# Sorting tokens to experts: integer compares, shifted prefix sums, one product on ScalarE, two peels issued later

## The reference

```python
xn = layernorm(x)                                   # 8 x 512 x 128
# attention: 8 heads of 16; differential: out1 - lam * out2, layernorm, times 0.2, Wo
s = attention(xn, Wq, bq, Wk, bk, Wv, bv, Wo, bo, lambdas, ln_w, ln_b)
# experts: the group h of a token comes from its first two numbers
h = mod((xn[:, 0] + xn[:, 1]).astype(int32), 8)     # cast cuts off towards zero
sel = [h, mod(h + 1, 8)]                            # two of eight experts, half weight each
f = mean over e in sel of (relu(xn @ W1[e] + b1[e]) @ W2[e] + b2[e])
out = x + s * silu(f)
```

## Time and profile before

| | us |
|---|---|
| median of 3 runs | 412.05 (411.11 to 412.3) |
| the profiled execution, its own time | 411.52 |
| its span, first to last instruction | 409.6 |
| PE busy in the span | 381.5 (93%) |
| DVE busy | 291.8 (71%) |
| ACT busy | 267.5 (65%) |
| POOL busy | 189.3 (46%) |
| mean granted TensorE clock | 0.991 of full |

### The profile page before, as it was taken

How to read it: one execution, slowest core, us unless ns; L and a number is a source line. 1 busy time by engine, 2 the same in 40 slices (tenths; PEclk the granted TensorE clock), 3 DMA queues, 4 the chain that set the end, 5 groups by cost and what they waited for, 6 DMA issues and landing times.

```text
span 409.6 us, 8427 instructions
## 1 busy us (share of the span) xinstructions
PE 381.5 (93%) x2576; PEld 248.3 (61%) x2576; DVE 291.8 (71%) x758; ACT 267.5 (65%) x667; POOL 189.3 (46%) x262
## 2 busy tenths in 40 slices
PE   4996989999999999999999999999999999999993
PEld 2353876565775667766665668765676667764321
DVE  7787996656686757766676767866686767866884
ACT  3581756666765776576666767676766668675783
POOL 7944203454456543565355532663573444541200
PEclk9996999999999999999999999999999999999999
DMA  7975953263216451265105640346136141216740
GB/s 263 343 230 112 242 196 91 80 206 105 79 37 191 111 195 21 79 190 168 46 27 170 189 140 18 136 121 197 48 127 216 22 169 47 81 26 213 230 159 26
DMA packets 36945, 54.75 MB, mean 134 GB/s; under 512 B 6724, under 2 KB 25141, under 8 KB 36903
## 3 DMA queue, kind: packets, MB, share of 16 engines
q1 hardware_dynamic: 31456, 46.94, 34.6%
q0 software_dynamic: 3296, 6.76, 7.8%
q10 hardware_dynamic: 2151, 0.53, 0.6%
HBM read 15.59 MB, written 6.75 MB: 55 GB/s over the span
## 4 chain that ended last, share of the span: by engine, by line
PE 74%; DVE 7%; DMA 5%; ACT 4%; SPq 4%; issue 4%; POOL 1%; ACTq 0%; DVEq 0%; POOLq 0%
PE ring L1393 14%; PE pv_bank L1327 13%; PE ring L1414 12%; PE score L1289 12%; PE exp L1314 10%; PE ring L1251 3%; DVE neg_max L1049 3%; DMA xs<-xn_rows,inverse 3%; SPq L532 2%; PE ring L1335 2%; PE ring L1255 1%; PE ring L1353 1%; PE ring L1276 1%; PE ring L1375 1%; PE score L1264 1%
## 5 line engine op out<-in xcount | busy, mean ns | idle before, releaser
L1049 DVE TENSOR_REDUCE neg_max<-score 128x1 f32<-128x512 f32 x256 | 169.0, 683 | 72.3 <-PE score L1289 66.7
L1289 PE MATMUL score<-ks,qs 96*128 96x512 bf16 x256 | 98.3, 386 | 6.3 <-DVE neg_max L1049 6.0
L787 ACT ACTIVATE probs<-exp 128x512 f32<-128x512 f32 x124 | 72.5, 605 | 36.3 <-PE exp L1314 32.3
L787 ACT ACTIVATE xin<-exp 128x512 f32<-128x512 f32 x120 | 69.7, 604 | 38.5 <-PE exp L1314 38.1
L1314 PE MATMUL exp<-qs,ks 99*128 99x512 bf16 x244 | 91.7, 380 | 0.1
L825 ACT ACTIVATE hT<-ring,pair 128x128 f32<-128x128 f32 x256 | 73.4, 377 | 13.0 <-PE ring L1393 11.9
L1414 PEld LDWEIGHTS ring<-w_sb,hT 128*128 128x128 f32 x568 | 73.5, 191 | 10.4 <-issue 3.5
L1414 PE MATMUL ring<-w_sb,hT 128*128 (+1 forms) x568 | 75.4, 275 | 0.9 <-ACT hT L825 0.9
L1393 PEld LDWEIGHTS ring<-xsT,pair 128*128 128x128 f32 x512 | 66.3, 191 | 14.6 <-issue 8.1
L1393 PE MATMUL ring<-xsT,pair 128*128 128x128 f32 x512 | 68.2, 276 | 1.7 <-issue 1.2
L684 POOL TENSOR_SCALAR tanh<-tanh 128x128 f32<-128x128 f32 x32 | 17.2, 536 | 95.5 <-ACT tanh L845 95.2
(11 more groups left out here) (198 smaller groups left out, 417.4 us busy)
## 6 DMA issues: line engine op xcount, KB each, us to landing
pair<-table SPq DMA_DIRECT2D x32, 580.0 KB
qs<-parts SPq DMA_DIRECT2D x42, 128.0 KB
ks<-parts SPq DMA_DIRECT2D x42, 128.0 KB
xin<-_attn_hidden_states_dram SPq DMA_DIRECT2D x8, 256.0 KB, 4.4
table<-in_L_ffn_W_dram SPq DMA_DIRECT2D x2, 1024.0 KB, 9.2
w_sb<-in_L_ffn_W_dram SPq DMA_DIRECT2D x8, 256.0 KB, 10.4
xn_rows<-xn SPq DMA_DIRECT2D x8, 256.0 KB, 3.0
table<-_attn_hidden_states_dram SPq DMA_DIRECT2D x8, 256.0 KB, 5.4
```

What stands on the lines that cost most here:

```text
L787: a.activation(prob(n), exp_banks[n][:, :], ACT.Exp, scale=SCALE).then_inc(exp_done, 1)
L1049: v.tensor_reduce(neg_max[:, b % 2, col:col + 1], score_bank[n % 2][:, :], AX.X, ALU.max, negate=True).then_inc(max_taken, 1)
L1289: t.matmul(score_bank[n % 2][:, :], qs[0:MAX_ROW, b % STK, hh, c * P:(c + 1) * P], ks[0:MAX_ROW, b % STK, hh, :], start=True, stop=True).t ...
```

## The change

In the list of steps: `peel 1 0 2` goes behind `score 4`, `peel 1 1 2` behind `score 5`; before, both stood ahead of `invert`. `tokens` goes ahead of `bias_copy` and has a part on ACT now. `extras` and `groups 2` go ahead of one score each on DVE. The extra tiles' `turn_tile` (f = 1 and 3 to 6) goes ahead of one or two steps on PE and ACT. `tanh` of the tiles f = 11, 12, 17, 18, 24, 25, 31, 32, 37 and 38 goes behind one `exp` on ACT, that of f = 21 behind `turn_z`. The moves of `split_max` and `load_y_init` pass no step of their own engines, so no engine's program changes by them.

In the grouping: the mean's part is subtracted from the pair's sum before the reciprocal deviation is there, so that one product is left behind it; the casts back to f32 are gone, and comparisons read the integers; `onehot` and `seen` lie one word further to the front, so that the scan reads one place off and gives the sum without the token's own one; `token[1]` is written by ACT. In the layer norm of batches 4 to 7, POOL subtracts the mean and multiplies, so `shift` isn't formed for them.

```diff
-PEEL_AT = (((-55.5, -55.3), (-55.4, -55.25)), ((-45.5, -45.3), (-45.4, -45.2)))
+PEEL_AT = (((-55.5, -55.3), (-55.4, -55.25)), ((-45.5, 4.5), (-45.4, 5.1)))
-TOKENS_AT = -45
+TOKENS_AT = -45.46
-EXTRAS_AT = 5.2
-GROUPS_AT = (9.05, 10.72, 13.05, 14.05)
+EXTRAS_AT = 4.7
+GROUPS_AT = (9.05, 10.72, 12.55, 14.05)
-TX, DX = 2.4, 3.2
+TX, DX = 3, 3.2
-INIT_AHEAD = 1.5
+INIT_AHEAD = 1.67
-SPLIT_MAX, TURN_MAX = 16.8, 18.9
+SPLIT_MAX, TURN_MAX = 16.5, 18.9
-TANH, GATE = 0.7, 1.84
+TANH, GATE = 1, 1.84
...
-        onehot = work[:, 512:768].rearrange("p (e t) -> p e t", e=EXP)
-        seen = work[:, 768:1024].rearrange("p (e t) -> p e t", e=EXP)
+        onehot = work[:, 511:767].rearrange("p (e t) -> p e t", e=EXP)
+        seen = work[:, 767:1023].rearrange("p (e t) -> p e t", e=EXP)
...
-                    if end < B:
+                    if first not in POOL_NORM:
...
-                    pool.wait_ge(shift_ready, 1 + [b >= end for _, end in LN_GROUPS].index(False))
+                    pool.wait_ge(rstd_ready, 1 + [b >= end for _, end in LN_GROUPS].index(False))
                     for t in range(C * b, C * b + C):
-                        last = g.tensor_scalar(xn[:, t, :], xin[:, t, :], rstd[:, t:t + 1], shift[:, t:t + 1],
-                                               ALU.mult, ALU.add)
+                        last = g.tensor_scalar(xn[:, t, :], xin[:, t, :], mv[:, t, 0:1], rstd[:, t:t + 1],
+                                               ALU.subtract, ALU.mult)
...
+                elif kind == "tokens":
+                    act.wait_ge(in_tile_ready, 1)
+                    a.activation(token[:, 1, :, :, :], in_tile, ACT.Copy, scale=row_of[:, 0:1]).then_inc(token_ready, 1)
...
                 dve.wait_ge(pair_summed, 1)
+                dve.wait_ge(rstd_ready, len(LN_GROUPS))
                 link(v.tensor_tensor(v01[:, :], v01[:, :], rstd[:, :], ALU.mult))
-                dve.wait_ge(shift_ready, len(LN_GROUPS))
-                link(v.scalar_tensor_tensor(v01[:, :], shift[:, :], 2.0, v01[:, :], ALU.mult, ALU.add))
...
-                link(v.tensor_copy(n_abs[:, :], whole_i))
-                link(v.tensor_tensor(over, n_abs[:, :], v_abs[:, :], ALU.is_gt))
-                link(v.tensor_tensor(n_abs[:, :], n_abs[:, :], over, ALU.subtract))
-                link(v.scalar_tensor_tensor(h[:, :], sign[:, :], -1.0, n_abs[:, :], ALU.add, ALU.mult))
-                link(v.tensor_copy(whole_i, h[:, :]))
-                link(v.tensor_scalar(whole_i, whole_i, EXP - 1, None, ALU.bitwise_and))
-                link(v.tensor_copy(h[:, :], whole_i))
+                link(v.tensor_tensor(over, whole_i, v_abs[:, :], ALU.is_gt))
+                link(v.tensor_tensor(n_abs[:, :], whole_i, over, ALU.subtract))
+                link(v.scalar_tensor_tensor(h_i[:, :], sign[:, :], -1.0, n_abs[:, :], ALU.add, ALU.mult))
+                link(v.tensor_scalar(h_i[:, :], h_i[:, :], EXP - 1, None, ALU.bitwise_and))
...
-                flat = work[:, 768:1024]
-                link(v.tensor_tensor_scan(flat, work[:, 512:768], zeros,
-                                          0.0, ALU.add, ALU.add))
-                v.tensor_tensor(seen[:, :, :], seen[:, :, :], onehot[:, :, :], ALU.subtract).then_inc(seen_ready, 1)
+                v.tensor_tensor_scan(work[:, 768:1024], work[:, 511:767], zeros,
+                                     0.0, ALU.add, ALU.add).then_inc(seen_ready, 1)
...
-                v.tensor_tensor(token[:, 0, :, :, :], in_tile, by_pair(ordinal[:, :], FT), ALU.mult)
-                v.tensor_scalar(token[:, 1, :, :, :], in_tile, row_of[:, 0:1], None, ALU.mult).then_inc(token_ready, 1)
+                dve.wait_ge(in_tile_ready, 1)
+                v.tensor_tensor(token[:, 0, :, :, :], in_tile, by_pair(ordinal[:, :], FT), ALU.mult).then_inc(token_ready, 1)
...
-                    v.tensor_tensor(v01[:, :], xin[:, :, 0], xin[:, :, 1], ALU.add).then_inc(pair_summed, 1)
-                    dve.wait_ge(rstd_ready, g + 1)
+                    link(v.tensor_tensor(v01[:, :], xin[:, :, 0], xin[:, :, 1], ALU.add))
                     dve.wait_ge(stats_ready, end)
-                    v.scalar_tensor_tensor(shift[:, tok], mv[:, tok, 0], -1.0, rstd[:, tok],
-                                           ALU.mult, ALU.mult).then_inc(shift_ready, 1)
+                    v.scalar_tensor_tensor(v01[:, :], mv[:, :, 0], -2.0, v01[:, :],
+                                           ALU.mult, ALU.add).then_inc(pair_summed, 1)
...
-                    pe.wait_ge(token_ready, 1)
+                    pe.wait_ge(token_ready, 2)
```

More of the change, by code:

```diff
@@ L306, in gated_attention_moe @@
         sign = sb("sign", [P, NT])
-        h = sb("h", [P, NT])
+        h_i = sb("h_i", [P, NT], I32)
         count = sb("count", [P, EXP])
@@ L429, in gated_attention_moe @@
         token_ready = sem("token_ready")
+        in_tile_ready = sem("in_tile_ready")
         slots_split = sem("slots_split")
@@ L860, in _ @@
             v.memset(zeros, 0.0)
+            v.memset(work[:, 767:768], 0.0)
             link(v.memset(va[:, :, :, :, HD:VW], 0.0))
@@ L896, in count_groups @@
                 v.tensor_scalar(sign[:, :], v01[:, :], 0.0, 2.0, ALU.is_ge, ALU.mult)
-                link(v.tensor_copy(n_abs[:, :], whole_i))
-                link(v.tensor_tensor(over, n_abs[:, :], v_abs[:, :], ALU.is_gt))
-                link(v.tensor_tensor(n_abs[:, :], n_abs[:, :], over, ALU.subtract))
-                link(v.scalar_tensor_tensor(h[:, :], sign[:, :], -1.0, n_abs[:, :], ALU.add, ALU.mult))
-                link(v.tensor_copy(whole_i, h[:, :]))
-                link(v.tensor_scalar(whole_i, whole_i, EXP - 1, None, ALU.bitwise_and))
-                link(v.tensor_copy(h[:, :], whole_i))
-                link(v.tensor_tensor(onehot[:, :, :], h[:, :].unsqueeze(1).to_broadcast([P, EXP, NT]),
+                link(v.tensor_tensor(over, whole_i, v_abs[:, :], ALU.is_gt))
+                link(v.tensor_tensor(n_abs[:, :], whole_i, over, ALU.subtract))
+                link(v.scalar_tensor_tensor(h_i[:, :], sign[:, :], -1.0, n_abs[:, :], ALU.add, ALU.mult))
+                link(v.tensor_scalar(h_i[:, :], h_i[:, :], EXP - 1, None, ALU.bitwise_and))
+                link(v.tensor_tensor(onehot[:, :, :], h_i[:, :].unsqueeze(1).to_broadcast([P, EXP, NT]),
                                      iota[:, 0:EXP].unsqueeze(2).to_broadcast([P, EXP, NT]), ALU.is_equal))
                 v.tensor_reduce(count[:, :], onehot[:, :, :], AX.X, ALU.add).then_inc(count_ready, 1)
-                flat = work[:, 768:1024]
-                link(v.tensor_tensor_scan(flat, work[:, 512:768], zeros,
-                                          0.0, ALU.add, ALU.add))
-                v.tensor_tensor(seen[:, :, :], seen[:, :, :], onehot[:, :, :], ALU.subtract).then_inc(seen_ready, 1)
+                v.tensor_tensor_scan(work[:, 768:1024], work[:, 511:767], zeros,
+                                     0.0, ALU.add, ALU.add).then_inc(seen_ready, 1)
             def make_slots(fill, shared):
@@ L945, in find_tokens @@
                 dve.wait_ge(slots_split, 1)
-                link(v.tensor_tensor(in_tile, by_pair(slot_tile[:, 0:NT], FT), over_pairs(columns[:, :, :], NT // 2), ALU.is_equal))
-                v.tensor_tensor(token[:, 0, :, :, :], in_tile, by_pair(ordinal[:, :], FT), ALU.mult)
-                v.tensor_scalar(token[:, 1, :, :, :], in_tile, row_of[:, 0:1], None, ALU.mult).then_inc(token_ready, 1)
+                v.tensor_tensor(in_tile, by_pair(slot_tile[:, 0:NT], FT), over_pairs(columns[:, :, :], NT // 2),
+                                ALU.is_equal).then_inc(in_tile_ready, 1)
+                dve.wait_ge(in_tile_ready, 1)
+                v.tensor_tensor(token[:, 0, :, :, :], in_tile, by_pair(ordinal[:, :], FT), ALU.mult).then_inc(token_ready, 1)
             def find_rows(q):
@@ L1014, in _ @@
                         continue
-                    tok = slice(C * first, C * end)
-                    v.tensor_tensor(v01[:, :], xin[:, :, 0], xin[:, :, 1], ALU.add).then_inc(pair_summed, 1)
-                    dve.wait_ge(rstd_ready, g + 1)
+                    link(v.tensor_tensor(v01[:, :], xin[:, :, 0], xin[:, :, 1], ALU.add))
                     dve.wait_ge(stats_ready, end)
-                    v.scalar_tensor_tensor(shift[:, tok], mv[:, tok, 0], -1.0, rstd[:, tok],
-                                           ALU.mult, ALU.mult).then_inc(shift_ready, 1)
+                    v.scalar_tensor_tensor(v01[:, :], mv[:, :, 0], -2.0, v01[:, :],
+                                           ALU.mult, ALU.add).then_inc(pair_summed, 1)
                 elif kind == "transpose_x" and s[1] not in PEELED:
```

## The result

The changed kernel takes 417.38 us (median, 416.79 to 417.61), the kernel before on the same chip 411.58. The ratio is 1.0146, 95% interval 1.0108 to 1.0184: slower by 5.8 us. The prediction had said 411.5 and a range to 413.6. The profiled execution of the changed kernel took 417.56, its span is 415.8.

A forecast was written before the change was run, and what follows sets the result against it. TensorE held 74% of the chain, but what counted was the time before about 70 us, with DVE rigid from 40 to 62. Terms -1.1 + 0.6 = -0.5 gave 411.0, as median 411.5; range 410.0 to 413.6.

The forecast's parts named there:

- The POOL part: POOL's layer norm of batches 4 and 5: two products fewer, gain at most 0.05 us.
- Removed on DVE, worth nothing: DVE's grouping ahead of make_slots: small instructions go, counts ready about 1 us earlier, but PE's count matmul sets it; gain 0.
- its cover: PE's peels of batch 0, said to hide the DVE and POOL savings; without them worth 1.5 us.
- The product on ScalarE: token[1]'s product moved from DVE to ACT at 26.72: takes 1.3 us there, ends DVE's at_row pieces 0.45 us earlier.
- the 1.04: Product on ACT and two peels moved behind the inversion: first gather starts and lands 1.04 us earlier, bounds 0.5 to 1.2.
- Rival (c): ACT's transfers start only after the late peel 1 1 1 copy and end at 37.4: 412.2 us, chance 0.12.
- The row-based forecast: ACT's fifteen transfers taken to start when they did before, from 29.33 to 36.92, with the peels' copies behind them.
- The clock: PE from 34 to 38 us: the moved first peel keeps full clock, so hidden 0 ends 1.2 us earlier.
- rival (b): PE's clock falls before turn_tile 0, second peel at half speed on the path, hidden 0 1.6 us later: 414.2, chance 0.16.
- The tanh moves: ACT's tanh in eleven tiles: gain 0, at best 0.5; tile 12's delays tile 14's gather, costing 0 to 0.85, taken 0.6.
- The sum without the form: Forecast total: -1.1 + 0.6 = -0.5 us against the profiled 411.52, so 411.0; as median 411.5.
- the first term: -1.1 us: hidden 0 ends earlier, taken between 1.2 at full clock and 0.9 if ACT's transfers delay the peel's copy.

The follow-up runs named there:

- the old form: Changed kernel with POOL's normalise of batches 4 to 7 put back to product and addition, shift formed again: 408.82 us against 409.97 of before, ratio 0.9974.
- the mended one: Changed kernel with minus_mean formed on POOL and added where the mean was subtracted: 410.86 us against 411.46 of before, ratio 0.9997.
- the second run with the old form: Changed kernel with POOL's product and addition back, run once more on another chip in more rounds: 408.95 us, ratio 0.9985.

## Why the prediction was wrong

**The step that failed is this:** "The POOL part is alike: two products fewer ... Gain at most 0.05." I costed the two small products that go and not the sixteen large instructions whose form changes. The trace of before has no subtraction of this shape on POOL, so the form was an operation that had to be bounded from both sides. I took it as the same operation, and the row of those sixteen instructions wasn't even among my rows. With double their 8.2 us POOL would have ended at 33, and by the earlier trace rows the stores about 3 us after that. That rival, some 5 us slower, could have been worked out from the trace, and it had no chance in the text. Measured, the form took 14.9 us in place of 8.2, the stores came last at the gather where the prediction had put the inversion, and the time grew by 5.8 us.

**Removed on DVE, worth nothing:** right for the execution it was read from, too general as a rule. With the steps gone, DVE waited for PE's counts ahead of `make_slots` for 0.3 to 1.3 us in five profiles (0.87 in the changed kernel) and not at all in three. With them in, PE waited for DVE by 0.4 and 0.6 us in two. PE's matmul of the counts stood anywhere from 20.05 to 22.10. The prediction itself said that both ends had met by chance; its cover was as uncertain. What the steps are worth in the median isn't shown.

**The product on ScalarE:** right in size. It started at 26.84 and took 1.33 us, against 1.3. It was in nobody's way, but only because the peels had moved. Its share of the gather is 0.47, from one execution of each; the 1.04 that I gave the edit together with the peels came out as 0.96 with the old form (31.45 to 30.49), 0.25 of it from PE being that much earlier at the counts.

**Rival (c), ACT's transfers behind the late copy:** wrong. ACT's queue in the changed kernel:

```profile
26.84 1.33 ACT L754 ACTIVATE probs<-hT,row_of 128x1248 bf16<-128x1248 bf16 x1
26.86 0.35 ACTq L719 DMA_DIRECT2D lams<-in_L_attn_lambda_q_dram  x1
```

The first of the transfers starts 0.02 us after the product, though five instructions of ACT's stand between them in its program and run only from 28.06 on. The row-based forecast had them at 29.3 or later. By the Trainium skill, "Advanced Engine Details and Errata" (Engine Queue Depths), ScalarE's queue holds 8 instructions, so its sequencer can hand over the product and the copies and go on; the trace agrees. The other half of that step held: a copy behind the transfers does wait for them. ACT in the run with the old form alone:

```profile
31.56 2.45 ACTq L732 DMA_DIRECT2D ks<-ones_bf  x3
34.06 0.69 ACT L778 ACTIVATE probs<-ring,qk_bias 128x512 bf16<-128x512 f32 x1 [4.57 <-PE ring L1260]
```

The profile names PE, but PE's matmul was over at 33.71 and the last transfer at 34.01. It cost nothing, as the first tile came only at 34.92. The transfers are thirteen, not the fifteen of the prediction.

**The clock:** the forecast of full clock from 34 to 38 held with the old form in some traces and not in others. Of the eight profiles with the old form or the mended one and the peels moved, three had 1.00 from 24 to 44 all the way (the first with the old form alone, and those with the product or the grouping back). In the others it fell for some microseconds between 28 and 38. In the second run with the old form the price was about 0.6 us and not 1.6, as the clock had mostly come back before the second peel (0.93 in the window from 36 to 38). In the changed kernel the gather was so late that the fall came behind it too, and there the second peel did run at half clock on the path, by the mechanism of rival (b).

**The tanh moves:** the gather of tile 14 was issued later as foreseen (129.09; by the 4.94 us of the shift it would have been 128.2), but it landed earlier too, and PE was 0.53 us less behind at that tile, not 0.6 more. So the lower bound, 0, was the right end for this term of the sum; that other traffic sets the landing is not shown. Over the whole stretch from tile 8 to the last, the shift against the profile of before grew by 1.2 us in the changed kernel. In the others it goes with the chip and not with the steps. On the two chips where the kernel before took 410.0 and 409.8 us, in all seven profiles it went down by 1.5 to 2.1 us, in those with the tanh moved (-2.1, -1.5, -2.1, -2.1) and in those without (-1.7, -1.8, -1.6) alike. On the two chips where it took 411.5, it changed by -0.2 to +1.2 in five profiles. So behind tile 8 profiles of two chips can't be compared to a microsecond, and the last 1.2 us of the changed kernel's loss have no shown cause.

**The sum without the form:** -0.5 us was forecast, from -1.1 at the start and +0.6 at tile 14; measured were -1.15 and -0.84 (medians against before), with intervals that reach from 0.9959 to 1.0008. So the rest of the change is worth between nothing and 1.7 us, about 1 by the medians. That fits the first term without the second, but the noise is too large to show it.

## What to carry to other kernels

An operation that only changes its form is an operation that the trace has not shown: find its row or bound it, and begin with the largest instructions that the edit touches, not with those that it removes. On GpSimd keep the negated value and add it; the subtraction took 1.8 times as long here. When a step is put on an engine with slack, look what stands behind it there: the product on ScalarE paid only with the peels behind the inversion.

## What the runs showed of the hardware

**GpSimd's subtraction.** On 128x128 f32 with two per-partition numbers: 457 ns (product, addition), 458 (addition, product), 814 (subtraction, product), 808 (product, subtraction), medians of 16 each. All profiles together have 448 to 474 ns for the forms with an addition and 808 to 826 for those with a subtraction, in both kernels and on several chips.

**GpSimd and VectorE get in each other's way.** The longest of the sixteen, 2.56 us, lies beside VectorE's three bf16 products. POOL and DVE of the changed kernel in order of time:

```profile
26.21 0.99 POOL L641 TENSOR_SCALAR xn<-xin,mv,rstd 128x128 f32<-128x128 f32 x1
...
27.19 2.56 POOL L641 TENSOR_SCALAR xn<-xin,mv,rstd 128x128 f32<-128x128 f32 x1
```

```profile
26.57 0.94 DVE L948 TENSOR_TENSOR probs<-hT,ordinal 128x1248 bf16<-128x1248 bf16 x1
27.44 2.51 DVE L953 TENSOR_TENSOR qs<-hT,grid 128x1536 bf16<-128x1536 bf16 x3
```

One GpSimd instruction ends 0.2 us before the three products do, at 29.75 and 29.95, and takes three times its usual time. The bf16 products of `find_tokens` took 0.94 us instead of the 0.81 that they take with GpSimd idle, the three others 2.51 instead of 2.42. With the old form GpSimd is done at 24.9, just before these products begin, so the slower form also moved it into the stretch where it is held up: some 1.8 of the 6.7 us that POOL lost. By the Trainium skill, "SBUF — State Buffer" (SBUF: two separate sides), GpSimd and a VectorE instruction with two inputs in SBUF share a pair of ports, and whichever starts first holds it for its whole length. GpSimd's 2.56 us agree with that; VectorE's loss of 0.13 us on a product is less than waiting for a whole instruction of GpSimd's would be. That the ports are the cause is argued, not shown.

**The clock of one program.** The same kernel was granted full clock in one execution and half for six microseconds in another, on another chip, with no difference in its program. On one chip, twelve executions of it had mean clocks from 0.982 to 1.000; those at 0.999 or more were 0.5 us faster at the median.

**Gathers.** Where PE waited for it, the first gather took 2.8 to 2.9 us from its issue to PE's first use when it went out at 36.9 or later (three profiles), and 4.1 to 6.1 us when it went out at 30.4 to 31.9 (nine profiles). On one chip two kernels with gathers at 30.38 and 30.49 had 6.1 and 4.4. No run here shows why.
